# One core's graph network: SyncE fetches the rows of eighteen tiles, one row per DMA, and GpSimd passes those tiles over

## The reference

```python
h = relu(layernorm(x))
for W, root, b in layers 1, 2, 3:            # relational convolution, 8 relations
    out = h @ root + b
    for r in range(8):
        msg = where(edge_type == r, (h @ W[r])[src], 0)
        out += segment_sum(msg, dst) / max(count of edges of type r at dst, 1)
    h = relu(out)
x = x + h
g = relu(layernorm(x))
h = relu((g + segment_sum(g[src], dst)) @ W1 + b1) @ W2 + b2
return x + batchnorm(h) + relu(layernorm(x))
```

## Time and profile before

| what | value |
|---|---|
| median of the runs | 1883.6 us |
| the profiled execution | 1885.77 us, span 1883.8 us |
| PE busy | 1277.2 us (68%) |
| DVE, ACT busy | 888.7 (47%), 645.7 us (34%) |
| POOL busy | 1612.1 us (86%) |
| mean granted clock of TensorE | 0.629 |
| DMA, mean of the span | 77 GB/s |

### The profile page before, as it was taken

The page is one execution under the profiler, slowest core; times in us unless marked ns, Lnnn a source line. Parts: engine busy times, 40 slices in busy tenths (PEclk is TensorE's granted clock), DMA queues, the critical chain, the costliest instruction groups (busy, mean ns, idle before and its releaser), DMA issues.

```text
span 1883.8 us, 18726 instructions
## 1 busy us (share of the span) xinstructions
PE 1277.2 (68%) x4614; PEld 863.5 (46%) x4614; DVE 888.7 (47%) x3270; ACT 645.7 (34%) x1146; POOL 1612.1 (86%) x2502
## 2 busy tenths in 40 slices
PE   7888665657476776666667666675566666667787
PEld 3564444434344554444444344454444444444554
DVE  5784754545442366757676666652222222122213
ACT  5404000000000376867677766732011011112123
POOL 5888888888888888888888888878888888888881
PEclk9987655555555655657565656575567675757678
DMA  7823332323232311213121312231111111111111
GB/s 240 288 81 90 102 116 71 112 72 103 80 90 62 97 46 45 90 46 90 45 90 45 91 45 79 58 96 45 46 45 45 46 45 45 46 45 46 46 46 45
DMA packets 70010, 144.25 MB, mean 77 GB/s; under 512 B 23487, under 2 KB 37048, under 8 KB 69896
## 3 DMA queue, kind: packets, MB, share of 16 engines
q0 software_dynamic: 39840, 81.67, 17.3%
q1 hardware_dynamic: 29624, 60.67, 8.9%
q10 hardware_dynamic: 432, 0.64, 0.1%
HBM read 100.23 MB, written 42.67 MB: 76 GB/s over the span
## 4 chain that ended last, share of the span: by engine, by line
POOL 75%; issue 11%; PE 9%; DMA 4%; DVE 1%; ACT 1%; another core or an unknown queue 0%; POOLq 0%; DVEq 0%; SPq 0%; ACTq 0%
POOL rows L1249 53%; POOL slow L1234 19%; DMA rows<-h_table,idx 3%; PE ps_agg L562 2%; POOL early L1239 2%; PE ps_agg L617 1%; PE ps_a L580 1%; PE ps_h L531 1%; POOL rows L1270 1%; PE ps_agg L591 1%; PE ps_a L669 0%; PE ps_a L649 0%; PE ps_a L603 0%; PE ps_h L669 0%; ACT early L733 0%
## 5 line engine op out<-in xcount | busy, mean ns | idle before, releaser
L1249 POOL DMA_INDIRECT rows<-h_table,idx x1183 | 1127.4, 953 | 199.7 <-issue 190.2
L562 PE MATMUL ps_agg<-sel,rows 128*128 128x64 f32 (+16 forms) x2780 | 734.6, 381 | 452.2 <-DMA rows<-h_table,idx 445.3
L562 PEld LDWEIGHTS ps_agg<-sel,rows 128*128 128x128 f32 x2780 | 638.7, 290 | 725.3 <-DMA rows<-h_table,idx 539.3
L964 DVE TENSOR_SCALAR sel<-iota,early,norm 128x64 f32<-128x64 f32 x1186 | 436.8, 430 | 474.4 <-PE ps_agg L562 451.9
L1234 POOL MEMSET slow<- 128x264 f32 (+1 forms) x1248 | 424.1, 340 | 0.7
L1060 DVE TENSOR_TENSOR early<-ps_a,early 128x300 f32 x416 | 197.5, 475 | 207.9 <-PE ps_a L649 160.9
L846 ACT ACTIVATE scratch<-scratch,ones 128x300 bf16<-128x300 f32 x416 | 222.6, 535 | 119.6 <-PE ps_a L649 96.6
L649 PE MATMUL ps_a<-scratch 128*128 128x300 bf16 x416 | 168.3, 405 | 113.5 <-issue 67.7
L852 ACT ACTIVATE scratch<-iota,code_lo 128x300 f32<-128x300 f32 x416 | 226.5, 545 | 12.5
L531 PE MATMUL ps_h<-w_all,xT 128*128 128x512 f32 x300 | 214.1, 831 | 6.6 <-issue 4.9
L942 DVE TENSOR_SCALAR_CACHE_REDUCE agg_s<-scratch,key_f 128x256 bf16<-128x256 int16 x416 | 194.8, 476 | 7.0 <-DMA scratch<-key_rows 5.5
(11 more groups left out here) (158 smaller groups left out, 760.5 us busy)
## 6 DMA issues: line engine op xcount, KB each, us to landing
h_table<-stage SPq DMA_DIRECT2D x65, 512.0 KB
rows<-h_table,idx POOLq DMA_INDIRECT x1183
scratch<-key_rows SPq DMA_DIRECT2D x26, 544.0 KB
h_table<-scratch SPq DMA_DIRECT2D x10, 512.0 KB
x_rows<-in_x SPq DMA_DIRECT2D x6, 256.0 KB, 6.3
w_all<-in_W SPq DMA_DIRECT2D x3, 512.0 KB, 6.6
x_table<-early SPq DMA_DIRECT2D x6, 256.0 KB, 2.3
out<-early SPq DMA_DIRECT2D x6, 256.0 KB
```

The costliest lines, as they stand in the source:

```text
L562: mm = nc.tensor.matmul(sums_of(L, k)[:, at:at + width], mine, sel[edges, G % SELS, in_window:in_window + width], start=False, stop=(t == ...
L964: done = nc.vector.tensor_scalar(mine, here, dst, weight, ALU.is_equal, ALU.mult)
L1249: pool.indirect_dma_start(rows[:, slot, :], None, table, bass.IndirectOffsetOnAxis(ap=column, axis=0)).then_inc(landed, 16)
```

## The change

Six whole tiles per layer (108, 166, 224, 282, 340, 398) are no longer gathered by POOL. Their 128 rows come by 128 DMAs of SP, each of one row of 512 bytes, into two own buffers. For that SP writes the six columns of `idx` to DRAM and reads them back as six lines; sixteen indices of a line are then loaded into registers by one instruction (a batch), eight batches a tile, spread over the tiles in between. PE waits for 128 completions at such a tile. POOL skips these tiles and their rests, and also the rests of the three short last tiles. Before the first batch of a tile SP waits until PE is through the tile that used the same buffer last.

```diff
+FETCHED = (108, 166, 224, 282, 340, 398)
+FETCH_FROM = 56
+LATER_FROM = 16
+FETCH_AHEAD = 4
+OWN_ROWS = 2
...
+    def fetch_at(L):
+
+        turns = [[] for _ in range(TILES)]
+        for n, t in enumerate(FETCHED):
+            since = FETCHED[n - 1] if n else (LATER_FROM if L else FETCH_FROM)
+            room = t - FETCH_AHEAD - since
+            for i in range(P // REGS):
+                turns[since + room * i // (P // REGS)].append((n, i))
+        return turns
...
+            elif G in FETCH_TILES:
+                turn = FETCH_TILES.index(G)
+                pe.wait_ge(s_own_row[turn % OWN_ROWS], 16 * P * (turn // OWN_ROWS + 1))
+                mine, edges = own_rows[:, turn % OWN_ROWS, :], slice(0, P)
...
+        def fetch_rows(sp, L, n, i):
+
+            turn = FETCHES * L + n
+            if i == 0 and turn >= OWN_ROWS:
+                sp.wait_ge(s_mm, cdiv(FETCH_TILES[turn - OWN_ROWS] + 1 - FORE, FREE))
+            found = [sp.alloc_register(f"row{L}_{n}_{p}") for p in range(REGS * i, REGS * i + REGS)]
+            sp.load(found, fetch_line[n:n + 1, REGS * i:REGS * i + REGS])
+            for p, x in enumerate(found, REGS * i):
+                row = sp.snap(x, donate=True, min_val=0, max_val=REL * N - 1)
+                sp.dma_start(own_rows[p:p + 1, turn % OWN_ROWS, :], h_tables[L][ds(row, 1), :]
+                             ).then_inc(s_own_row[turn % OWN_ROWS], 16)
...
+                    if b == SP_BRANCH:
+                        sp.wait_ge(s_idx, 1)
+                        for n, t in enumerate(FETCHED):
+                            sp.dma_start(fetch_cols[n:n + 1, :].rearrange("o p -> p o"), idx[:, t:t + 1]
+                                         ).then_inc(s_fetch_out, 16)
+                    if b == LAST:
+                        sp.wait_ge(s_fetch_out, 16 * FETCHES)
+                        sp.dma_start(fetch_line[:], fetch_cols[:]).then_inc(s_fetch_in, 16)
                 load_w()
...
+                sp.wait_ge(s_fetch_in, 16)
+                for L in range(GIN):
+                    turns = fetch_at(L)
+                    for t in range(TILES):
+                        c = t // CHUNK + 3
+                        if L == 0 and t % CHUNK == 0 and 2 + len(CHUNK_BEHIND) <= c < CHUNKS:
+                            sp.wait_ge(s_match, CHUNK // BATCH * (c - 1))
+                            load_chunk(sp, c)
+                            if c == END_CHUNK:
+                                fetch_ends(sp, 0)
+                        for b in range(BLOCKS):
+                            if L < LAST_REL and turn_of(L, b, 1) == t:
+                                store_rows(sp, L + 1, b)
+                        if L and t == LATER_FROM:
+                            fetch_ends(sp, L)
+                        if L == 0 and t == FETCH_FROM:
+                            wait_table(sp, 0)
+                        for n, i in turns[t]:
+                            fetch_rows(sp, L, n, i)
...
-                        if G in END_TILES:
-                            rest_a_while(G, PAUSE)
+                        if G in END_TILES or G in FETCH_TILES:
                             continue
```

More of the change, by code:

```diff
@@ L1 @@
+import itertools
 from contextlib import ExitStack
@@ L202, in gnn_kernel @@
     assert 0 < ENDS <= REGS and AHEAD_OF_PE <= SLOTS
+    FETCHES = len(FETCHED)
+    FETCH_TILES = [TILES * L + t for L in range(GIN) for t in FETCHED]
+    assert HEAD < FETCH_FROM < FETCHED[0] and FETCHED[-1] < TILES - 1 and FETCHED[0] > LATE_TILES
+    def fetch_at(L):
[6 more added lines that the diff above has]
+        return turns
     def gathered(G):
-        return sum(1 for g in range(FORE + (G - FORE) % SLOTS, G + 1, SLOTS) if g not in END_TILES)
+        return sum(1 for g in range(FORE + (G - FORE) % SLOTS, G + 1, SLOTS) if g not in END_TILES + FETCH_TILES)
     key_rows = nc.dram_tensor("key_rows", (1, HALO + COLS * P), I16, kind="Internal").ap()
@@ L220, in gnn_kernel @@
     assert LATE_PARTS[-1][2] + KEY_BANK <= P * SUM_BLOCKS[0][0]
+    fetch_cols = nc.dram_tensor("fetch_cols", (FETCHES, P), I32, kind="Internal").ap()
     x0_table = nc.dram_tensor("x0_table", (NP, D), F32, kind="Internal").ap()
@@ L234, in gnn_kernel @@
         rows = sb("rows", [P, SLOTS, D])
+        own_rows = sb("own_rows", [P, OWN_ROWS, D])
+        fetch_line = sb("fetch_line", [FETCHES, P], I32)
         sel = sb("sel", [P, SELS, SPAN])
@@ L428, in gnn_kernel @@
         s_end = sem("s_end")
+        s_fetch_out = sem("s_fetch_out")
+        s_fetch_in = sem("s_fetch_in")
+        s_own_row = [sem(f"s_own_row{n}") for n in range(OWN_ROWS)]
         s_mm = sem("s_mm")
@@ L1178, in _ @@
                         load_chunk(sp, c)
-                load_w()
[L1180 to L1184, removed]
-                    for b in range(BLOCKS):
-                        if CHUNK * (c - 3) <= turn_of(0, b, 1) < CHUNK * (c - 2):
-                            store_rows(sp, 1, b)
@@ new lines, in _ @@
+                    if b == LAST:
+                        sp.wait_ge(s_fetch_out, 16 * FETCHES)
+                        sp.dma_start(fetch_line[:], fetch_cols[:]).then_inc(s_fetch_in, 16)
+                load_w()
+                sp.wait_ge(s_fetch_in, 16)
[17 more added lines that the diff above has]
+                            fetch_rows(sp, L, n, i)
+                    for b in range(BLOCKS):
+                        if L < LAST_REL and turn_of(L, b, 1) >= TILES:
+                            store_rows(sp, L + 1, b)
@@ L1228, in _, with rest_a_while @@
             pool.wait_ge(s_x0, 16 * GROUPS)
[L1230 to L1235, removed]
+            rests = itertools.count()
+            def rest_a_while(words):
+                n = next(rests)
+                if n % 2 == 0 and n:
+                    pool.wait_ge(s_rested, n // 2)
+                done = nc.gpsimd.memset(slow[:, n % 2, 0:words], 0.0)
+                if n % 2 == 1:
                     done.then_inc(s_rested, 1)
@@ L1241, in _ @@
                                         ).then_inc(s_fore_row[t // BATCH], 16)
-                rest_a_while(t, HEAD_PAUSE)
+                rest_a_while(HEAD_PAUSE)
             pool.wait_ge(s_idx, 1)
@@ L1274, in _ @@
                             gather(L, G % SLOTS, idx[:, t:t + 1], s_row[G % SLOTS])
-                        rest_a_while(G, PAUSE)
+                        rest_a_while(PAUSE)
             with pool.Else():
```

## The result

The changed kernel took 1867.8 us (median of 4 runs, 1862.3 to 1869.2), the kernel before 1883.4 (4 runs, 1880.6 to 1884.6): a ratio of 0.9914 with the 95% interval 0.9894 to 0.9933, so 15.6 us faster. The profiled execution took 1862.3 us with a span of 1860.2. Later the same kernel was also 13% slower, in one session of measurements; that is told with the experiments.

A forecast was written before the change was run, and what follows sets the result against it. POOL, always in its own list, was taken as the bound. Gross 27.1 us less 4, 1.5, 2.0, 0.5 and 0.4 left 18.7: 1864.9 against the median, stated as 1866 for row-cost risk; range 1855 to 1892.

The forecast's parts named there:

- The gross gain: POOL's list: eighteen gathers with rests at 1.45 us, 26.1 us, plus two border rests, 1.0 us; 27.1 us together.
- The row and the load: SP's list: 0.475 us a row (0.32 to 0.62), 1.10 us a sixteen-register load (0.47 to 1.93); batch 8.7 us.
- Tile 108: Layer 0: last batch stands behind a store, PE stands 13.5 us, POOL loses 4 us at tile 120 (2 to 9).
- PE needs 0.28 + 1.94 (line 603) + 0.28: Layer 0, after tile 108's rows land at 200.1: PE's work before POOL's tile 120 can go, about 203.
- Tile 166: Layer 0: SP still late from 108, by little; 0.4 us for all other tiles, 4 to 6 more at 0.50 a row.
- The set-up: Writing and reading back index columns before layer 0's gathers: costed at nothing, as SP issues stores faster than blocks are made.
- The two places in layer 1: Tile 224, where PE stands 4 us and POOL loses 1.5; border of layers 1 and 2, 2.0 us lost.
- The rival "SP becomes the bound": SP's list overflows from 0.555 us a row, late at layers 0 and 1's fetched tiles; 1937 or from 1888 up; chance 0.20.
- The other estimate beside it: SP's load by the Trainium skill's 200 ns a register: a tile takes 89.3 us, the time some 1945 us.

The follow-up runs named there:

- the run with the other order: Changed kernel with all eight batches of layer 0's tile 108 ahead of the store with turn 95: 1860.1 us, ratio 0.9882 to the kernel before.

## Why the prediction was right, and where its steps were not

The forecast of 1866 us holds for the session that decided it (1867.8) and for the two after it (1863.7 and 1859.9, gains of 18.6 and 21.8). Point by point:

**The gross gain: right.** A skipped tile brings its turn of 1.45 us, shown alone in layer 2 (8.5 for six). POOL's skipping without SP's rows brings 23.3 of the 27.1; of the rest, 3.0 us are the set-up in its profile, where the first gather of table 0 starts at 86.4 in place of 83.4.

**The row and the load: near.** The row was taken at 0.475 us and is 0.421; the load at 1.10 and is 1.23, more behind a store. A batch is 8.0 in place of 8.7. The estimate left the gaps of the five-row fetch at 0.06 us for each instruction, and they are less: (0.409 - 0.037 - 0.029 - 0.225) / 3 = 0.04.

**Tile 108: right place, price too low.** PE was to stand 13.5 us and stood 14.5; POOL was to lose 4 and lost 6.1. The step that failed is "PE needs 0.28 + 1.94 (line 603) + 0.28": behind the stand the same four matmuls took 3.73 us, and the sums took 0.69 for two and 0.95 for four matmuls in place of 0.56 for four. Here the stand on PE cost twice, once as itself and once in the lower clock behind it. In the times the price of tile 108 rests on the run that only skips, 4.8 us faster; the run with the other order has no wait there and does not confirm it.

**Tile 166: its overlap was misjudged, and it cost nothing.** The prediction let SP make up its delay by its 10 us to spare for each tile, so that little would be left at 166. But behind tile 108 SP had to wait, ahead of its next chunk, for DVE, which does the matching and had itself stood 16.0 us behind PE. DVE's first instruction behind its stand, and SP's wait, in the profile after:

```profile
208.82 0.35 DVE L963 TENSOR_SCALAR scratch<-iota,late 128x256 f32<-128x256 f32 x1 [16.02 <-PE ps_a L634]
...
SPq L1148 <- DVE agg_s L973: 10.3, 1, 10.3
```

So PE's stand at 108 passed over DVE back to SP and used up the spare time, and PE stood 5.5 us at tile 166. POOL's lead hid it.

**The set-up: cost at nothing, and it costs 1 to 5 us.** SP and POOL, by timeline, in the profile after:

```profile
41.17 3.06 SPq L1225 DMA_DIRECT2D fetch_cols<-idx  x6
...
84.96 0.95 POOL L1310 DMA_INDIRECT rows<-h_table,idx  x1 [2.30 <-DMA h_table<-scratch]
```

The six column DMAs take 3.06 us of issue. The last store of table 0 was issued at 73.3 in the profile of before and at 78.3 here, 5.0 later, and the first gather starts 1.5 us later (1.1 to 5.4 in the profiles of the first two sessions with this set-up). The cover that the prediction named, that SP issues stores faster than blocks are made, was thinner than it read. Here that store lands at 84.1; in the kernel with the unused buffers it lands at 80.4, 3 us before the first gather at 83.4. So there were 3 us of cover for a delay of 5. In the run with the columns behind that store the wait is gone. Another 1.9 us go between tiles 64 and 80 in the profile after and in its repeat: gather 66 waits 2.5 us for PE. That is only in part the change's, for it waits 0.6 in the profile of before and 1.7 in that of the kernel with the unused buffers.

**The two places in layer 1: did not come.** The sum took 1.5 us off at tile 224 and 2.0 at the border. Both steps rest on PE lagging in layer 1 and on the border wait of 4.73 us, and these waits go with conditions that stood in that execution and in the third session, not with the kernel. In the profiles after, PE does not lag, tile 224 is not waited for, and against that execution the border shows a gain of 5 us. How much of it is in the medians is open; two profiles of kernels that took the same time as before do not have the wait.

So the total came out partly by luck, as errors that compensate: 108 and the set-up cost 3.6 us more than reckoned (2.1 and 1.5), the places in layer 1 cost 3.5 less.

**The rival "SP becomes the bound": refuted in two sessions, true in the third.** The prediction put the turning point at 0.555 us a row, and gave for it the waits at every fetched tile of layers 0 and 1 and a lower price in layer 2. With 0.42 nothing of it came; with 0.72 it did, at eleven of the twelve tiles and for less in layer 2, at about its price. The other estimate beside it, 3.2 us for a load of sixteen registers, came in no session: it was 1.2 in all of them. That a row can be held up stood in the maxima of the earlier trace rows, and the prediction kept it in its bounds. What holds SP up is not shown, and no run was made to find it; whether anything outside this kernel was at work on the chip is not known. Three things are shown: the hold-ups are on the same instructions that ran clean in two sessions; they come with issue waits on PE, in the kernel before too; and they nearly cease while PE stands. It can't be the chip alone, if its number means what it says, for the second session had none. The instruction queues carried the same amount in both sessions (129 or 130 packets on the larger one).

## What to carry to other kernels

Work moved from a bound engine to an idle sequencer is worth what the first engine no longer does, if the second arrives in time: reckon its list per period, item by item, and keep room. Here a row of 0.42 us, where 0.555 was the limit, was enough for 1%, and it was lost more than ten times over where the row rose to 0.72, while the kernel before lost 1.2% under the same conditions. So weigh a small gain against the case in which the helper is held up, and read the maxima of its instructions and the issue waits of all engines as the sign of it. A wait that stands in one profile of a kernel is not yet the kernel's: compare with a second profile before a step rests on it.

## What the runs showed that was not expected

- The same program took 1864 us in one session and 2151 in another, all six runs there between 2142 and 2165. The kernel before went from 1882 to 1904 us.
- SP's hold-ups in the third session go with what PE does: 0.43 us a row while PE stands, 0.80 while it works, in one trace, and nearly so in two more. So a stand on PE that waits for SP shortens itself.
- Sixteen registers in one load cost SP 1.23 us, two 0.471, one 0.467: most of a load is fixed, and a further register adds about 0.05.
- In the first two sessions SP, issuing rows, lost 0.37 us about every 43 rows; from one such loss to the next it was 126 to 130 of its instructions nearly every time, or twice that.
- A stand of PE came back to SP: PE's 14.5 us at tile 108 stopped DVE's matching, and SP then waited 10.3 us for it.
